# A four-part model kernel on one core: convolution folded into the projection, gate on GpSimd, last product turned, queries and keys split in two single-pass parts and sent through DRAM

## The reference, cut to what matters

```python
x = x + S(_layernorm(x)); x = x + G(_layernorm(x)); x = x + T(_layernorm(x)); x = x + F(_layernorm(x))

# S: a state space block, 256 channels, 16 states each
x_ssm, res = split(x @ W_in.T)
x_conv = silu(conv4(x_ssm) + conv_b)            # 4 taps back in time, one channel each
A_d = exp(softplus(x_conv)[..., None] * -exp(A_log));  h_t = A_d * h + x_conv ** 2
out = (x_conv * sum(h) * silu(res) + D * x_conv) @ W_out.T
# G: a gate over 8 experts: residual of a projection per expert, softmax, top 2, weighted sum of 8 products
# T: attention, 16 heads of 8 + 4 (rotary) features
scores = Q @ K.T;  causal;  softmax(scores / sqrt(12)) @ V;  @ W_O
# F: h = silu(x @ w1.T * s1) * (x @ w2.T * s2);  h = gelu(h @ h1.T * s);  h = gelu(h @ h2.T * s)
out = (h @ w3.T) * s3
```

## Time and profile before

| | us |
|---|---|
| median of 3 runs | 1786.47 |
| lowest and highest run | 1783.78, 1786.57 |
| the profiled execution, its own time | 1786.55 |
| its span, first to last instruction | 1781.5 |
| VectorE busy | 1519.0 |
| TensorE busy | 1502.4 |
| ScalarE busy | 1284.4 |
| GpSimd busy | 1103.6 |
| mean granted TensorE clock | 0.976 |

### The profile page before, as it was taken

How to read it: one execution, slowest core, us unless ns; L and a number is a source line. 1 busy time by engine, 2 the same in 40 slices (tenths; PEclk the granted TensorE clock), 3 DMA queues, 4 the chain that set the end, 5 groups by cost and what they waited for, 6 DMA issues and landing times. The chain is left out here.

```text
span 1781.5 us, 24641 instructions
## 1 busy us (share of the span) xinstructions
PE 1502.4 (84%) x8039; PEld 807.3 (45%) x8039; DVE 1519.0 (85%) x2837; ACT 1284.4 (72%) x2176; POOL 1103.6 (62%) x987
## 2 busy tenths in 40 slices
PE   4245788888889888888888888888898799999997
PEld 1122343333334333333433334333434588888886
DVE  6899999999999999999999999997331688988883
ACT  5665888988989898898989889895555454444441
POOL 5884776868577686867768586775122255555552
PEclk9996999999999999999999999999999699999998
DMA  4000000000000000000000000000200000000000
GB/s 136 0 1 0 18 13 7 19 1 19 1 19 16 4 19 1 18 1 19 17 3 19 1 19 1 18 15 5 84 3 17 1 7 12 13 13 13 13 13 19
DMA packets 14543, 27.41 MB, mean 15 GB/s; under 512 B 3837, under 2 KB 4550, under 8 KB 13898
## 3 DMA queue, kind: packets, MB, share of 16 engines
q1 hardware_dynamic: 14410, 25.79, 5.2%
HBM read 9.00 MB, written 4.19 MB: 7 GB/s over the span
## 5 line engine op out<-in xcount | busy, mean ns | idle before, releaser
L616 POOL TENSOR_TENSOR sum_fast<-sum_fast,state_fast 128x512 f32<-128x512 f32 x448 | 573.9, 1281 | 78.1 <-DVE state_fast L598 38.0
L598 DVE TENSOR_TENSOR_SCAN state_fast<-state_fast,bank 128x512 f32<-128x512 f32 x512 | 602.7, 1202 | 0.7 <-ACT bank L567 0.7
L1008 ACT ACTIVATE prob_fast<-bank 128x1024 f32<-128x1024 f32 x320 | 326.0, 1020 | 122.1 <-PE bank L992 111.7
L992 PE MATMUL bank<-stacks_fast 64*128 64x512 f32 (+3 forms) x2048 | 361.4, 462 | 50.0 <-ACT prob_fast L1008 46.6
L583 ACT ACTIVATE state_fast<-chan_all_kept,neg_a_fast 128x512 f32<-128x512 f32 x512 | 340.1, 713 | 10.6 <-POOL sum_fast L616 8.5
L1052 POOL TENSOR_SCALAR_AFFINE_SELECT prob_fast<-prob_fast 128x512 f32<-128x512 f32 x256 | 159.9, 636 | 293.6 <-ACT prob_fast L1008 292.1
L992 PEld LDWEIGHTS bank<-stacks_fast 64*128 64x128 f32 x2048 | 170.7, 185 | 250.0 <-ACT prob_fast L1008 150.8
L1069 PE MATMUL bank<-prob_fast,v_ext_fast 128*32 128x512 f32 (+3 forms) x2048 | 177.7, 442 | 8.1 <-POOL prob_fast L1052 7.5
L670 PE MATMUL bank<-resid_m_fast,xnt_g_fast 128*128 128x512 f32 x256 | 137.2, 637 | 34.5 <-DVE gate_fast L751 33.1
L701 PE MATMUL bank<-we_t_fast,xnt_g_fast 128*128 128x512 f32 x256 | 133.7, 633 | 2.5 <-DVE own_fast L822 2.5
L1545 ACT ACTIVATE full_fast<-bank,sh_kept 128x512 f32<-128x512 f32 x64 | 44.1, 689 | 122.4 <-PE bank L1455 122.4
(11 more groups left out here) (204 smaller groups left out, 2596.1 us busy)
## 6 DMA issues: line engine op xcount, KB each, us to landing
stacks_fast<-parts_fast SPq DMA_DIRECT2D x128, 64.0 KB
stacks_fast<-rest_fast SPq DMA_DIRECT2D x128, 32.0 KB
out_x<-f_out_fast SPq DMA_DIRECT2D x16, 256.0 KB, 2.0
x_res_kept<-in_x SPq DMA_DIRECT2D x1, 2048.0 KB, 13.7
chan_all_kept<-in_h_t SPq DMA_DIRECT2D x2, 1024.0 KB, 7.0
x_res_kept<-in_x SPq DMA_DIRECT2D x1, 1024.0 KB, 9.3
chan_all_kept<-in_w_t SPq DMA_DIRECT2D x3, 256.0 KB, 3.9
x_res_kept<-in_x SPq DMA_DIRECT2D x2, 256.0 KB, 3.3
```

The costliest lines, as they stand in the source:

```text
L598: dve.tensor_tensor_scan(h[:], h[:], self.banks[0][:], 0.0, ALU.mult, ALU.add).then_inc(self.v_scan.sem)
L616: pool.tensor_tensor(total[:], total[:], h[:], ALU.add).then_inc(self.p_sum.sem)
L992: ins = pe.matmul(self.scores(b, step)[:, c:c + SEQ - P * kt], rows[:, 1, h // 2, P * kt:P * kt + P], rows[:, 0, h // 2, P * kt:SEQ], star ...
L1008: act.activation(self.probs[u % 2][:, i * 1024:(i + 1) * 1024], self.scores(b, 5 * g + n)[:], ACT.Exp, scale=SCALE).then_inc(self.a_prob.sem)
```

## The change

1. **Convolution in the projection.** At the start VectorE multiplies the projection by each of the four taps into `taps`. A half's convolution is then four f32 matmuls that accumulate in bank 1, the later ones shifted by one to three tokens. L500 and the three instructions of L536 are gone; one VectorE instruction adds the bias and clips, out of the bank. The taps arrive as two loads of 256 KB more in the first set of loads.
2. **Gate by GpSimd.** The clipped second projection goes to a fourth place, `raw`; GpSimd multiplies it with its silu in place of L546. The bank is free after the clip. The clipped value stands in for the bank's.
3. **Queries and keys in two parts.** `parts` becomes fp32r and VectorE subtracts it from the bank to give `parts_lo`; GpSimd does the same for the rotary rows (a copy and a subtraction more). In `stacks` a head has 48 rows: queries as high, low, low, high and keys as high, low, high, low. One fp32r pass then gives all four cross products. `sp_rows` writes the rows to DRAM (`rows_q`, `rows_k`, two buffers each; 10 transfers) and reads the stacks from there (16 transfers, each 24 rows of 8 KB). The code of `pe_scores` is the same.
4. **Last product turned.** w3 is now the weight side, and 512 tokens move: 8 matmuls for each sequence. ScalarE scales by s3 (per partition now), TensorE turns it back with four transposes, VectorE adds x out of the bank. L1616 is gone.
5. **Orders.** PERIOD, F_PERIOD, all of TIMES and EDGES are new; some small tensors share memory. As an example, within one sequence the last step of `act_t_proj` stands at 187,711 before and at 165,013 after, the first of `pe_scores` at 203,934 and 203,707.

```diff
-PERIOD, F_PERIOD = 78858, 24000
+PERIOD, F_PERIOD = 72494, 24942
...
# pe_s_head
-            pe.matmul(bank[:], w[:, ct * P:(ct + 1) * P], xnt[:], start=True, stop=True).then_inc(self.t_s_in.sem)
+            for back in range(TAPS):
+                ins = pe.matmul(bank[:, back:], self.taps[:, ct, back], xnt[:, 0:SEQ - back], start=(back == 0),
+                                stop=(back == TAPS - 1))
+            ins.then_inc(self.t_s_in.sem)
...
# act_s_head
-            act.activation(tmp, bank[:], ACT.Identity, bias=self.conv_b[:, ct:ct + 1],
-                           scale=self.conv_w[:, ct, TAPS - 1:TAPS]).then_inc(self.a_s_tap.sem)
...
# dve_s_head
-            for back in range(1, TAPS):
...
-                dve.scalar_tensor_tensor(
-                    out=tmp[:, back:], in0=bank[:, 0:SEQ - back], scalar=self.conv_w[:, ct, TAPS - 1 - back:TAPS - back],
-                    in1=tmp[:, back:], op0=ALU.mult, op1=ALU.add).then_inc(self.v_s_conv.sem)
...
-            dve.tensor_scalar(xc, tmp, -40.0, None, ALU.max).then_inc(self.v_s_conv.sem)
+            dve.tensor_scalar(tmp, bank[:], self.conv_b[:, ct:ct + 1], -40.0, ALU.add, ALU.max).then_inc(self.v_s_conv.sem)
...
-            dve.tensor_scalar(gate, bank[:], -40.0, None, ALU.max).then_inc(self.v_s_clip.sem)
-            yield
-            dve.wait_ge(self.a_s_sig2.sem, self.a_s_sig2.at(b, 3 * ct + 2))
-            dve.tensor_tensor(gate, bank[:], gate, ALU.mult).then_inc(self.v_s_gate.sem)
+            dve.tensor_scalar(raw, bank[:], -40.0, None, ALU.max).then_inc(self.v_s_clip.sem)
...
# pool_s_head
+            pool.wait_ge(self.a_s_sig2.sem, self.a_s_sig2.at(b, 3 * ct + 2))
+            pool.tensor_tensor(gate, raw, gate, ALU.mult).then_inc(self.p_s_gate.sem)
...
# dve_t_proj
+            dve.tensor_tensor(self.parts_lo[:, i], bank[:], parts[:, i].bitcast(F32), ALU.subtract).then_inc(self.v_t_lo.sem)
...
# pool_t_proj
+        pool.tensor_copy(hi[:], full[:]).then_inc(done.sem)
+        pool.wait_ge(done.sem, done.at(b, 1))
+        pool.tensor_tensor(self.rest[1][:].bitcast(F32R), full[:], hi[:].bitcast(F32), ALU.subtract).then_inc(done.sem)
...
# sp_rows
+        for at, src in ((DH, hi), (DQK + DH, lo), (2 * DQK + DH, hi)):
+            sp.dma_start(q[s, at:at + DR].rearrange("d h p c -> (d h p) c"), src[0:NQ]).then_inc(out_rot.sem, 16)
...
+            for at, src in ((0, hi), (DQK, lo)) + (((2 * DQK, hi),) if i == 0 else ()):
+                sp.dma_start(rows[s, at:at + DH].rearrange("d h p c -> (d h p) c"), src).then_inc(out_rows[i].sem, 16)
...
+                for parity in range(2):
+                    for twice in range(2):
+                        r, at = 64 * parity + 2 * DQK * twice, 0 if i else DQK * twice
+                        sp.dma_start(stacks[r:r + 2 * DQK, i, cols].bitcast(F32),
+                                     rows[s, at:at + 2 * DQK, 2 * parity + half]).then_inc(moved.sem, 16)
...
# pe_f_out
+        for mt in range(MT):
+            for i in range(parts):
+                ins = pe.matmul(banks[6][:], w["w3_t"][:, mt * DM:(mt + 1) * DM], self.f_h2[s][mt][:, i],
+                                start=(mt + i == 0), stop=(mt == MT - 1 and i == parts - 1))
...
+            ins = pe.transpose(banks[6][:, k * P:(k + 1) * P], self.f_y[:, k * P:(k + 1) * P], self.ident[:])
...
# act_f_out
+        act.activation(self.f_y[:], self.banks[6][:], ACT.Identity, scale=self.s3[:, 0:1]).then_inc(self.a_f_out.sem)
...
# dve_f_out
-        dve.tensor_tensor(out[:], banks[6][:].rearrange("p (k f) -> p k f", k=NT),
-                          self.s3_row[:].unsqueeze(1).to_broadcast([P, NT, DM]), ALU.mult).then_inc(self.v_f_out.sem)
...
-        dve.tensor_tensor(out[:], out[:], self.x(b), ALU.add).then_inc(self.v_f_out.sem)
+        dve.tensor_tensor(out[:], banks[6][:].rearrange("p (k f) -> p k f", k=NT), self.x(b), ALU.add).then_inc(self.v_f_out.sem)
```

427 lines of the change are left out of this document (234 added, 193 removed).

## The result

The changed kernel takes 1762.45 us, median of four executions (1757.57 to 1763.94), where the kernel before takes 1785.12 beside it: a ratio of 0.9868, 95% interval 0.9845 to 0.9892. It is faster, by 1.3%; 1672.5 was forecast, with a range of 1640 to 1730 that does not hold it. Its profiled execution took 1763.9 us with a span of 1761.5, 20.0 less than before.

What follows compares the result with a forecast made beforehand. VectorE, busy 96% of a 77.8 us period, was taken to bound the steady part. From 1786.55 us, -80 (steady part), +5 (start), -20 (tail) and -19 (phase two) gave 1672.5 us, range 1640 to 1730.

Steps and rivals of the forecast that it cites:

- VectorE's work: Steady period: instructions removed and added make VectorE's busy time 4.8 us less, from 74.7 to 69.9 us.
- phase two: Turned last product: 1.2 us less for each of 16 sequences, 19 us less in all (21 to 10).
- the upper of my bounds: Single-pass score step on TensorE: 0.23 us with two heads side by side, 0.47 one behind the other.
- VectorE stays the bound: Steady part: period 72.0 us from a floor of 71.0, fifteen intervals giving 80 us less; chance 0.70.
- The upper end of 75.0: Steady period: the long end of the range 71.0 to 75.0 us, where new orders leave VectorE idle 5 us.
- rival C: Steady part: TensorE's granted clock falls below 0.82 and it becomes the bound; period 78.5, about 1780 us; chance 0.04.
- the argument against it: TensorE's clock: the ramp's 0.86 came with whole stretches of waiting, which should not arise in the interleaved steady period.
- rival B: Steady part: steps wait for ones too early in other queues; period 75 and more, 1726 us; chance 0.16.
- The start: First sequence: two added loads and tap products, slower first convolution, some instructions gone; 5 us more (2 to 10).
- The tail: Behind phase one's last scan: shorter score steps, against 8 us over DRAM; 20 us less (35 less to 5 more).
- The way over DRAM: From keys to scores: a write and a read replace one transfer, 8 us, covered in the steady part by other scans.
- Rival D: SP's ordered transfers become the bound, 86 us for each sequence at 3.3 us each; 1888 us; chance 0.05.

Runs made afterwards that it cites:

- four passes: The kernel after, its score products reading the same 48 rows as plain f32, so each takes more passes: 1826.9 us, ratio 1.0241.
- kernel 2: The kernel before with single-pass scores over its own 12 rows (rounded) and the last product of phase two turned, with phase two's new times: 1728.5 us.
- its folded form: kernel 2 with the convolution folded into the projection and nothing else: 1752.4 us.
- the kernel with one tap: The kernel after with one product for each half of the convolution instead of four, the three delayed taps left out: 1726.1 us.
- the three score variants: The kernel after as it is (1762.5 us), with each score product issued twice (1770.4 us), and with scores in four passes (1826.9 us).
- kernel 5: Every part of the change in the orders of the kernel before, new steps put in beside what they follow: 2016.2 us.
- kernel 1: The kernel before with only its score products read as fp32r in a single pass, without the second part: 1755.7 us.
- kernel 4: kernel 2 with the gate product on GpSimd, the second one 34.7 us later in its list, and the convolution folded: 1768.7 us.
- 5 with small transfers: kernel 5 with its row transfers over DRAM cut to 8 of 512 columns, as many transfers and waits: 1806.2 us.
- small transfers: The kernel after with its row transfers over DRAM cut to 8 of 512 columns, as many transfers, waits and issues: 1765.6 us.

## Why the prediction was wrong, point by point

**Right, or nearly.** VectorE's work (69.9 forecast, 71.25 in the period shown and 70.9 in the mean of ten; it fell by 3.7 us where I had 4.8: the terms that I listed make 4.7, and overlaps that go with six instructions make the fall smaller, not larger), ScalarE's (67.5; 66.3), GpSimd's (61.6; 60.4, as the copy took 0.61 us and not the 1.26 I had put down), TensorE's at full clock (58.9; 59.4), phase two (-19; -22.4). A score step takes 0.43 us to the next start at full clock (494.61 to 495.04 us on TensorE's timeline; in the slow stretch shown, from 593.83 to 594.55, 0.72): two heads go one behind the other, at the upper of my bounds, 0.47, and not at the 0.3 that I took. With four passes they still overlap.

**The step that failed: "VectorE stays the bound", so that a period is its work and 2 us.** I took "96% busy" for "costs what it works". For the kernel before that was nearly so: single-pass scores alone bring periods of 75.2 us, at VectorE's floor. But with the convolution folded in, the next thing was not a floor some four us below. It was a chain through TensorE, ScalarE and GpSimd, whose steps stand in a written order: 3.0 us less on VectorE made the period 2.2 us longer (kernel 2 and its folded form, at the same clock), 2.8 us more on VectorE cost the kernel after 0.3, and 6.4 us less on TensorE gave it 3.0. I had priced TensorE's 6.4 us more at nothing because its sum, 58.9 of 72 us, fitted. The upper end of 75.0 for the period was exceeded by 3.2. How the 6.2 us between 72.0 and 78.2 divide between clock and order stays open: every means to raise the clock was itself work in the chain, and no second set of orders was tried.

**The clock, rival C at 0.04.** Its figures (period 78.5, some 1780 us) are nearest to what came, 78.2 and 1762, but that is luck. Its condition was a mean below 0.82 and a TensorE that is bound by its sum; the mean of the ten periods is 0.89. And the level of the clock alone doesn't tell the period: the kernel with one tap has 75.3 us at 0.85, kernel 2 76.2 and its folded form 78.4 at 0.92, four passes 82.4 at 0.98. What did fail is the argument against it, that only whole stretches of waiting lower the clock: 69.89 busy us of 78.85 came with 0.85, where 67.66 of 77.80 had 1.00 before. A busy share counts slow products as work; put at full clock it is 75% against 87%. The Trainium skill's rule (TensorE: Matmul & The Clock Gate, section on the HAM clock gate), that activity releases the throttled state, agrees with the three score variants (0.887, 0.926, 0.953).

**Orders, rival B at 0.16.** It was right that a step stands too early in another queue (the gate product ahead of the masks is one in the old orders), wrong in its price: 3 us a period over the forecast, where this one move cost 4.8. It named ScalarE or GpSimd as what VectorE would wait for; the largest waits are for TensorE (2.7 and 1.5 us a period), ScalarE's is 2.0.

**The start, +5 against +6.1.** The number was right by luck. In the old orders the folded convolution leaves the end of the first sequence's scans at 68.1 to 70.7 us, where it is 70.1 before; the loads and products that I priced cost next to nothing there. The 6 us come with the new orders (68.8 in kernel 5, 76.2 in the kernel after).

**The tail, -20 against -2.3.** The count of 2.6 sequences of scores behind the last scan was about right, 2.75 on TensorE's timeline (3.0 in the kernel after). The terms written down, 16 and 7 less and 8 more, make 15 and not 20. The single pass gave 8 to 17 us, 15.6 in kernel 1; the rows with hardly any bytes took 8.3 back (kernel 4 to 5 with small transfers, low parts included), as priced; the bytes, which I had at nothing, took 29.7 more, and the new orders gave 27.7 of them back. I read the 38.7 us between projection and scores in the new times, where 16.2 stood, as cover. It did cover the bytes.

**The way over DRAM, 8 us.** From the keys' low part to the first score it is 28 us in the old orders, 14 to 16 of them without the bytes. I took landings of single transfers and thought the bytes cheap; but the three writes of 256 KB held SP for 2.8 to 4.5 us each. Rival D (0.05) had the right resource; in the kernel after small transfers change nothing (1765.6 us), as the orders leave room. The queue's packets took 21.9% of 1761.5 us, 386, where they took 93; with 46 of those for the 12.8 MB that fell away, that is 21 us for each sequence over 16 engines, where I took 18. How many engines carry a transfer, that sum doesn't tell; a stretch of kernel 5 in which reads of the stacks are under way, behind its writes, does (columns as above):

```profile
578.00:590.00 12.00, 1.87 (x4) 0.79 (x4) 0.49 (x1) 1.03 (x2) 1.89 (x2) 0.53 0.77 158
```

A DMA share of 0.77 is near 12 of 16. The rule of the Trainium skill (DMA: Bandwidth & Descriptors, section on why a DMA increments its semaphore by 16), 12 engines for 24 rows, agrees with it. At 158 GB/s the 3.1 MB of reads alone take 20 us, and the queries' writes hold SP for 11.2 us ahead of them, so the estimate of 25 for all 5 MB was still too low.

## What to carry to other kernels

A busy share near 100% tells which engine sets the period, not what the period becomes when its work shrinks: price the second chain before crediting a gain. Taking work off TensorE can lower its clock; what that costs depends on which product it falls on, and the mean doesn't tell. Try the cheapest part alone first, here a cast of the score rows and one turned product, which beat the whole change. And when a change moves steps in a static order, split the time at the work that sets the pace: the end of S seemed to make the tail 36.5 us longer, when only the mark had moved.

## What the runs showed that I had not expected

- One order, same work, periods of one kernel: 75.43 us at a granted clock of 1.00, 76.10 at 0.93, 80.65 at 0.92. The kernel before takes 1785 us at a mean clock of 0.957 and 1784 at 0.978.
- Products with zero weights, 8.5 us a sequence, took the mean clock from 0.887 to 0.910; the same time in doubled score products took it to 0.926.
- 256 KB writes to `rows_q` land in 8.9 us and hold SP for up to 4.46 us, equal ones to `rows_k` behind them in 3.3 and 0.65. With 8 of 512 columns the issue takes 0.4 us.
- In single-pass products of 64 rows two heads go one behind the other; in four passes they overlap: 1.06 us a step with 12 and with 48 rows.
